# A fused decoder layer: one hand-written order of steps for all engines becomes one order for each engine, and an 8-bit cast moves from GpSimd to VectorE

## The reference, cut to what matters

```python
# x, ctx: (32, 256, 256); cells: (32, 1, 256, 1), integers 0..63
q, k, v = x @ Wq, x @ Wk, x @ Wv            # 16 query heads, 4 key/value heads, 64 wide
q, k = rope(q), rope(k)
a = softmax(q @ k.T / 8 + alibi)            # 16 heads, 256 x 256 each
x1 = layernorm(x + (a @ v) @ Wo)
# windowed cross attention: 16 heads of 16, windows of 64 looking one window back, cells must match
qx, kx, vx = proj(x1), proj(ctx), proj(ctx) # each with its own layernorm
o = softmax(where(mask, rope(qx) @ rope(kx).T / 4, -max)) @ vx
x2 = layernorm(x1 + proj(o))
# feed forward with ternary weights and activations rounded to 8 bits per token
h = gelu(quant8(x2) @ Wg.T) * (quant8(x2) @ Wu.T)
y = layernorm(x2 + quant8(h) @ Wd.T)
```

## Time and profile before

| | us |
|---|---|
| median of 3 runs (2417.35 to 2425.89) | 2421.6 |
| the profiled execution, its own time | 2430.4 |
| the profiled execution, its span | 2428.3 |
| TensorE busy in the span | 2162.9 (89%) |
| VectorE busy | 2030.8 (84%) |
| ScalarE busy | 1647.4 (68%) |
| GpSimd busy | 1500.9 (62%) |

### The profile page before, as it was taken

The page is one execution under the profiler, slowest core; times in us unless marked ns, Lnnn a source line. Parts: engine busy times, 40 slices in busy tenths (PEclk is TensorE's granted clock), DMA queues, the critical chain, the costliest instruction groups (busy, mean ns, idle before and its releaser), DMA issues. The chain is left out here.

```text
span 2428.3 us, 57742 instructions
## 1 busy us (share of the span) xinstructions
PE 2162.9 (89%) x19280; PEld 1652.3 (68%) x19370; DVE 2030.8 (84%) x8045; ACT 1647.4 (68%) x4609; POOL 1500.9 (62%) x1614
## 2 busy tenths in 40 slices
PE   4689999999999999999999999999999999999864
PEld 3566767677777767777776777777677777767642
DVE  4778788888888888888888888888888898888864
ACT  2366677776677777767777776777776677777642
POOL 2346566666766666666666666666666666666543
PEclk9899999999999999999999999999999999999986
DMA  3110010101110010111001001110100110010100
GB/s 99 61 30 25 19 36 25 34 25 28 34 34 25 26 34 25 28 34 34 25 26 34 25 27 34 34 25 26 34 25 27 34 34 25 26 34 23 29 14 9
DMA packets 85395, 74.62 MB, mean 31 GB/s; under 512 B 18544, under 2 KB 79344, under 8 KB 85104
## 3 DMA queue, kind: packets, MB, share of 16 engines
q1 hardware_dynamic: 85104, 70.93, 10.6%
HBM read 45.72 MB, written 8.39 MB: 22 GB/s over the span
## 5 line engine op out<-in xcount | busy, mean ns | idle before, releaser
L1152 ACT ACTIVATE prob<-prob,nmax 128x256 f32<-128x256 f32 x1024 | 508.5, 500 | 215.7 <-DVE nmax L879 215.5
L1240 POOL TENSOR_TENSOR prob<-prob,precs 128x512 f32<-128x512 f32 x512 | 524.0, 1042 | 200.3 <-DVE precs L886 197.8
L879 DVE CUSTOM_DVE_ANT_0 prob<-bank,alibi 128x256 f32<-128x256 f32 x1024 | 372.2, 420 | 51.7 <-PE bank L579 51.0
L475 PE MATMUL bank<-ident,prob 128*128 128x128 f32 x2048 | 315.8, 277 | 18.7 <-ACT pT L1159 13.9
L1159 ACT COPY pT<-bank 128x512 f32<-128x512 f32 x512 | 299.8, 586 | 40.0 <-PE bank L475 39.9
L1176 ACT ACTIVATE px<-px,nmx 128x128 f32<-128x128 f32 x1024 | 313.5, 391 | 19.1 <-DVE nmx L988 17.0
L475 PEld LDWEIGHTS bank<-ident,prob 128*128 128x128 f32 x2048 | 236.4, 141 | 81.5 <-issue 39.9
L598 PE MATMUL bank<-pT,v_sb 128*64 128x256 f32 x2048 | 252.0, 388 | 5.9 <-DVE xtok L899 5.2
L988 DVE CUSTOM_DVE_ANT_0 px<-bank,mask 128x128 f32<-128x128 f32 x1024 | 225.9, 286 | 20.0 <-PE bank L658 11.2
L487 PE MATMUL bank<-w_hi,x_hi 128*128 128x256 f32 (+1 forms) x512 | 193.3, 377 | 50.8 <-DVE by_sin L860 26.8
L1305 POOL TENSOR_SCALAR hq<-hh 128x1024 bf16<-128x1024 f32 x64 | 233.1, 3642 | 5.6
(11 more groups left out here) (209 smaller groups left out, 6042.6 us busy)
## 6 DMA issues: line engine op xcount, KB each, us to landing
raw<-in_xT SPq DMA_DIRECT2D x32, 256.0 KB, 2.7
kx_tok<-in_ctx SPq DMA_DIRECT2D x32, 256.0 KB, 3.0
xtok<-in_x SPq DMA_DIRECT2D x32, 256.0 KB, 2.8
raw<-in_ctxT SPq DMA_DIRECT2D x32, 256.0 KB, 3.4
kx<-k_sin SPq DMA_DIRECT2D x256, 32.0 KB, 2.0
vs<-vx SPq DMA_DIRECT2D x64, 128.0 KB, 2.3
out_y<-x SPq DMA_DIRECT2D x32, 256.0 KB, 2.1
cellk<-in_cell SPq DMA_DIRECT2D x32, 64.0 KB, 3.6
```

The lines of the kernel that those rows point to most:

```text
L475: last = nc.tensor.transpose(bank[:, n * P:(n + 1) * P], src, ident[:])
L879: v.tensor_tensor_reduce(out=prob[:, (2 * p + q) % SLOTS, c, :], in0=psum[SCORES[c]][:, q * L:(q + 1) * L], in1=alibi[:, p % 2, :], scale= ...
L1152: nc.scalar.activation(prob[:, (2 * p + q) % SLOTS, c, :], prob[:, (2 * p + q) % SLOTS, c, :], ACT.Exp, bias=nmax[:, i:i + 1], scale=-1.0, ...
L1240: g.tensor_tensor(prob[:, n % SLOTS, :, :], prob[:, n % SLOTS, :, :], precs[:, 2 * n:2 * n + 2].unsqueeze(2).to_broadcast([P, 2, L]), ALU. ...
```

## The change

1. `HEAD`, `BODY` and `TAIL` become dictionaries with one list for each of `sp`, `pe`, `dve`, `act`, `pool`. A step's part on one engine may now stand before or after another step's part, whatever the others do. `order(engine)` strings the three together; 27 repetitions of the body as before.
2. The order itself is new on every engine.
3. `HC`, the subtraction, clip and bf16 write of the second 8-bit rounding, is issued by VectorE.
4. The credits are gone: counts start at zero, and a wait on a batch that does not exist becomes a wait on a semaphore `begun` that GpSimd sets once.
5. ScalarE runs one `Exp` on four constants before its list.

The queries' rope (`Q`) and every other instruction stay as they are.

```diff
-CREDIT = 2
-BODY = [
-    (2, 'R', 12), (2, 'R', 13), (2, 'S', 7), (2, 'W', 0), (2, 'load_ctx'), (3, 'TX', 1, 1), (3, 'SX', 3), (2, 'mask'),
...
+BODY = {
+    "pe": [
+        (4, 'D', 0), (3, 'TX', 1, 1), (3, 'SX', 3), (2, 'O', 2), (3, 'OX', 0), (3, 'TX', 2, 0), (2, 'S', 7), (2, 'T', 12),
...
+        (2, 'NX'), (1, 'T', 3), (1, 'S', 3), (0, 'K'), (3, 'G', 1), (1, 'qT', 3), (2, 'QX'), (3, 'U', 1), (1, 'O', 0),
+        (2, 'KXT'), (3, 'G', 2), (1, 'T', 4), (3, 'U', 2), (0, 'Q', 0, 1), (1, 'T', 5), (1, 'S', 4), (3, 'G', 3),
+        (1, 'T', 6), (2, 'QXT'), (3, 'U', 3), (0, 'Q', 1, 1), (1, 'T', 7), (1, 'S', 5), (2, 'SX', 0), (1, 'O', 1),
+        (1, 'T', 8), (3, 'HT', 0), (1, 'T', 9), (2, 'SX', 1), (2, 'TX', 0, 0), (1, 'S', 6), (1, 'T', 10), (2, 'TX', 0, 1),
+        (1, 'W', 0), (2, 'SX', 2), (1, 'T', 11), (2, 'TX', 1, 0), (0, 'qT', 0),
+    ],
+    "dve": [
+        (2, 'R', 12), (3, 'SX', 2), (2, 'R', 13), (1, 'qT', 0), (4, 'D', 0), (3, 'SX', 3), (2, 'mask'), (4, 'HC', 1),
...
+        (2, 'YS'), (1, 'qT', 2), (3, 'U', 0), (1, 'S', 3), (2, 'NX'), (1, 'R', 6), (0, 'K'), (1, 'qT', 3), (1, 'R', 7),
+        (2, 'QX'), (3, 'U', 1), (2, 'KXT'), (3, 'HS', 0), (3, 'U', 2), (0, 'Q', 0, 1), (1, 'S', 4), (3, 'U', 3),
+        (2, 'QXT'), (1, 'R', 8), (1, 'O', 0), (1, 'S', 5), (3, 'HC', 0), (1, 'R', 9), (1, 'R', 10), (2, 'SX', 0),
+        (0, 'Q', 1, 1), (3, 'HS', 1), (1, 'O', 1), (1, 'R', 11), (2, 'SX', 1), (1, 'S', 6), (3, 'HT', 0), (1, 'W', 0),
+    ],
...
+HEAD = {
+    "sp": [
+        (0, 'first', 0), (0, 'first', 1), (0, 'first', 2), (0, 'loads', 1), (0, 'load_xT'), (0, 'load_ctx'),
+        (0, 'tables', 0), (0, 'loads', 0), (0, 'tables', 1), (1, 'load_xT'), (0, 'load_cell'), (0, 'loads', 2),
...
+    "dve": [
+        (0, 'first', 0), (0, 'first', 1), (0, 'first', 2), (0, 'prep', 0), (0, 'tables', 0), (0, 'K'), (0, 'Q', 0, 1),
+        (0, 'prep', 1), (0, 'prep', 2), (0, 'prep', 3), (0, 'Q', 1, 1), (0, 'kT'), (0, 'prep', 4), (0, 'qT', 0),
+        (0, 'qT', 1), (0, 'Q', 0, 2), (0, 'wo_split'), (0, 'Q', 1, 2), (0, 'prep', 5), (1, 'K'), (0, 'tables', 1),
+        (0, 'S', 0), (0, 'prep', 6), (0, 'R', 0), (0, 'R', 1), (0, 'S', 1), (0, 'R', 2), (0, 'prep', 7), (0, 'R', 3),
...
+FILL = max(x[0] for steps in BODY.values() for x in steps) + 1
+def order(engine):
+    return HEAD[engine] + [(it - lag, *step) for it in range(FILL, B) for lag, *step in BODY[engine]] + TAIL[engine]
+def freed(sem, bank, steps, n):
+    for batch, *step in reversed(steps[:n]):
         if holds(step[0], bank) or (step == ["prep", 5] and bank == 7):
             name, k = EMPTIED[tuple(step)]
-            return sem[name], (batch + CREDIT) * COUNT[name] + (k + 1)
-    return sem["x_hi"], 1
+            return sem[name], batch * COUNT[name] + k + 1
+    return sem["begun"], 1
...
         def at(name, batch, k=0):
-            return sem[name], (batch + CREDIT) * COUNT[name] + (k + 1)
+            count = batch * COUNT[name] + k + 1
+            return (sem[name], count) if count > 0 else (sem["begun"], 1)
...
-            for name, n in COUNT.items():
-                pe.sem_inc(sem[name], CREDIT * n)
             pe.wait_ge(pool_consts, POOL_CONSTS)
-            run(HEAD)
-            for it in range(FILL, LAST):
-                run(BODY, it)
-            run(TAIL)
+            run(order("pe"))
...
+                    elif kind == "HC":
+                        t, = args
+                        dve.wait_ge(*at("hq_shift", b, t))
+                        dve.wait_ge(*at("HT_mm", b, t - 1))
+                        v.tensor_scalar(hq[:], hh[:, t, :], MAGIC, 127.0, ALU.subtract, ALU.min).then_inc(sem["hq_ready"], 1)
...
+            act.wait_ge(pool_consts, 4)
+            nc.scalar.activation(psums[:, 0:1], minus_half[:, 0:1], ACT.Exp)
+            run(order("act"))
...
-                    elif kind == "HC":
-                        t, = args
-                        pool.wait_ge(*at("hq_shift", b, t))
-                        pool.wait_ge(*at("HT_mm", b, t - 1))
-                        g.tensor_scalar(hq[:], hh[:, t, :], MAGIC, 127.0, ALU.subtract, ALU.min).then_inc(sem["hq_ready"], 1)
...
+            pool.sem_inc(sem["begun"], 1)
```

More of the change, by code:

```diff
@@ L398, in one, with run @@
                 return ap[bass.ds(b, 1)]
-            def run(part, it=0):
-                for place, b, *step in batches(part, it):
+            def run(steps):
+                for place, (b, *step) in enumerate(steps):
                     kind, args = step[0], step[1:]
@@ L539, in run @@
                         pe.wait_ge(*at("x_lo", b))
-                        pe.wait_ge(*freed(sem, bank, part, place, it))
+                        pe.wait_ge(*freed(sem, bank, steps, place))
                         for t in range(TT):
@@ L1095, in _, with run @@
             dve.wait_ge(pool_consts, POOL_CONSTS)
-            run(HEAD)
-            for it in range(FILL, LAST):
-                run(BODY, it)
-            run(TAIL)
+            run(order("dve"))
         @block.scalar
         def _(act):
-            def run(part, it=0):
-                for place, b, *step in batches(part, it):
+            def run(steps):
+                for place, (b, *step) in enumerate(steps):
                     kind, args = step[0], step[1:]
@@ L1326, in _ @@
                                 pattern=[[-1, P]], channel_multiplier=1).then_inc(pool_consts, 1)
-            run(HEAD)
-            for it in range(FILL, LAST):
-                run(BODY, it)
-            run(TAIL)
+            run(order("pool"))
 def rope_table(n, dim, first):
```

109 lines of the change are left out of this document (60 added, 49 removed), and 270 rows, old and new, of tables (BODY, HEAD, TAIL).

## The result

The changed kernel takes 2326.2 us (median of 4 runs, 2325.2 to 2331.8), the kernel before 2423.7 beside it (4 runs, 2417.4 to 2426.2): ratio 0.961, 95% interval 0.958 to 0.963. The forecast was 2328. The profiled execution has a span of 2324.6 us where the one before had 2428.3, 103.7 us more.

The account below looks back on a forecast made before the run. TensorE and VectorE, both close to full, were taken to set the period through waits on each other or GpSimd. Body 73 + head 12 + tail 9 = 94 us off 2430.4 gives 2336, less 8.8: 2328 us, range 2285 to 2400.

Parts of the forecast that it names:

- The cast's price: HC on VectorE: 0.69 us per cast, 2 per batch, so 1.4 us more VectorE work per period.
- The hold of 0.3 us per period: VectorE's casts in the body, blocked by GpSimd instructions under way: 0.3 us per period taken, 2.5 at most.
- held by GpSimd: Rival: GpSimd always holds VectorE's cast, 58 us back, 2386 us; within the 2350 to 2410 group given 0.29.
- VectorE's busy time: Body, per period: 61.95 us plus 1.4 for the casts and 0.3 for their holding.
- TensorE's waits: Body: 4.7 us per period; HC's 1.56 and most others go, 0.9 stays (0.3 for xqT, 0.6 for XQ).
- VectorE's waits: Body: 7.3 us per period become about 3.9: ktok's 2.67 goes, W 0 costs 1.5, four others 0.6 each.
- The period: Body: 70.8 us falls to 68.0, from TensorE's 66.8 and VectorE's 68.85; gain 73 us, bounds 31 and 117.
- The head: Start and first batches: 12 us gained, between -12 and 30; first matmul at 17 us, 8 us from batches 1 to 5.
- The tail: Last batches, from 2271 us on: waiting for four casts mostly goes, 9 us gained, between 3 and 15.
- Sum: Whole kernel: 73 + 12 + 9 = 94 us gained, 2336 from the profiled 2430.4, 2328 as the runs' median.
- Slower: Rival in VectorE's body queue: it becomes the bound with waits unchanged, period 72.2 us, 2437 us; chance 0.09.
- No change: Rival: VectorE's waits of about 5.5 us per period, head and tail giving nothing; within 0.3%, chance 0.04.

Follow-up runs that it names:

- cast_only: The kernel before with only the cast HC moved from GpSimd to VectorE; common order, credits and start as before: 2457.6 us, ratio 1.014.
- cast_back: The changed kernel with HC back on GpSimd, directly behind HS in its list; all other orders as changed: 2409.4 us, ratio 0.994.
- mask_beside_pool: The changed kernel with the mask's four instructions moved directly behind HS 0 in VectorE's body list: 2400.9 us, ratio 0.990.
- cast_at_once: The changed kernel with each batch's first cast (HC 0) directly behind HS 0 in VectorE's body list: 2411.5 us, ratio 0.995.
- cast_behind_u: The changed kernel with each batch's first cast seven steps earlier on VectorE, behind HS 0 and U 2: 2359.5 us, ratio 0.973.

## Why the prediction was right

The time and the sign came out. The steps, in the prediction's order:

- **The cast's price.** Forecast 0.69 us from a line through two rows; measured 0.687 in the body. The hold of 0.3 us per period is not there in the kernel after, 24.7 us in 36 casts: its list puts the casts where GpSimd stands idle. One of the 64 began with a GpSimd instruction under way, outside the body, and took 1.54. The runs with the cast elsewhere show it in full, 1.52 us. So the rival *held by GpSimd* was not a matter of how busy GpSimd is, as I argued from a mean, but of one place in the list.
- **VectorE's busy time.** Forecast 61.95 + 1.4 + 0.3, measured 61.87. I had not seen that the mask's instructions, 2.14 us per period before, would be 1.07 after. Before, they ran beside a normalisation on GpSimd; below. Either half of the change ends that: they are short in cast_only and in cast_back as well.
- **TensorE's waits.** `hq` went, as forecast. `xqT` and `XQ`, for which I kept 0.9 us, went as well. In their place are 1.2 us for ScalarE's copies of `pT`, 0.4 for `qx` and 0.3 for `xtok`, which I didn't look for: I had set TensorE's list beside VectorE's, and not beside ScalarE's. 2.0 in place of 0.9.
- **VectorE's waits.** The `ktok` one went, 2.7 of the 7.3. The forecast of 1.5 us at `W 0` was wrong (0.1), and of the four of 0.6 at `D 1`, `SX 3`, `PO` and `KV 1` only 0.25 us at `SX` is there. Against that 2.0 us for scores and 1.9 for ScalarE's sums. 4.8 against 3.9, led by the scores and not by `W 0`, and 0.2 below the 5 that the prediction named as its own refutation.
- **The period.** 68.0 forecast, 68.2 measured, but the way to it was unsound: the mean of TensorE's 66.8 and VectorE's 68.85. Each engine's busy time, waits and short gaps fill one and the same period, so two sums that differ by 2 us mean that terms are wrong in one or both, and a mean does not mend them. TensorE's waits were put 1.1 us too low; VectorE's work 1.5 to 1.8 too high and its waits 0.9 too low. That these errors and the mean met at 68 was luck.
- **The head.** 12 us forecast, 26.0 measured, the term most off. The first matmul came at 14.25, not 17 (the load was issued at 4.01 and had landed by 12.04, not at 15). And for batches 1 to 5 I took 2 us less per batch; the starts of `kk_hi` are 66.3 us apart, where they were 72.0 before. The runs divide it: the start without credits gives 10 to 15, the common order kept but with the cast on VectorE takes 6 to 8, the separate orders give 17. The first scores come late, at 63.4 us (before 45.9), as forecast. The copy of batch 1's `V` is still 1.9 us later than before, and that of batch 2 is 15.7 earlier: 17.6 of the head's 26 us lie between these two.
- **The tail.** 9 forecast, 10.8 measured. **Sum:** 67 + 26 + 11 = 104, where 73 + 12 + 9 = 94 was forecast; the medians differ by 97.5, and the body's miss of 6 and the head's of 14 are opposite in sign. The time of 2328 came out by luck beyond that. The prediction took the gain from the profiled execution's 2430.4, which gives 2336, and then 8.8 off because the median before lay that much lower. After, the profiled execution took 2326.7 and the median is 0.5 below it. So the gain was 10 us too small and the 8.8 too large, and the two cancelled.
- ***Slower*.** I gave it 0.09 and put its place in VectorE's queue. The mechanism exists: cast_only is it, at 2457.6. VectorE's waits are 7.7 us per period there, above the 5.9 that the prediction named; it held them unlikely because the 2.67 for `ktok` go, which they did, and others came, 1.9 for ScalarE's `oT_hi` and 1.36 for `hh`. By TensorE's rows the loss in the body is the clock's, which the prediction has nowhere.
- ***No change*.** It put this at 5.5 us of waits. By its own floor it is 70.8 - 64.95 = 5.9, as under *slower*.

**How the change works**, by the runs: the cast on VectorE gives 36 us if it isn't put directly behind its own hand-over, and costs 33 if it is. The start gives 10 to 11. Separate orders give 55.8 and also a place for the cast. Orders and cast are not additive: with the cast on GpSimd, the new orders have TensorE wait for the normalisations behind it.

**Left open.** Whether the separate orders need the cast on VectorE: cast_back had it directly behind `HS` on GpSimd and nowhere else. Which of the remaining 2.0 us of TensorE's waits can be had; the 1.2 for `pT` are ScalarE's, and no run moved a single step of ScalarE. How the head's 17 us divide among the moved preparation steps wasn't tried. Nor was any engine's list put back alone with the others as they are, but for ScalarE's.

## What to carry to other kernels

Add up busy time and waits of the engine whose work the change leaves alone; the sum shows where a period's time went, and a rise of its busy time says to look at its clock. It closes for other engines as well, so it does not say who is the bound. For each instruction that is put on another engine ask two things: does it stand directly behind the step that hands its input away, and which step of the full engine waits for what is queued behind it. A part of a change that loses alone may be what makes the rest pay, so test it in a second place before it is dropped.

## What the runs showed of the hardware

**VectorE and GpSimd hold each other.** The mask in the kernel before, then in the kernel after:

```profile
820.90 2.04 POOL L1240 TENSOR_TENSOR prob<-prob,precs 128x512 f32<-128x512 f32 x2
821.47 0.50 DVE L972 CAST cellqf<-cellq 128x2 f32<-128x2 int32 x1
822.00 1.35 DVE L975 SCALAR_TENSOR_TENSOR mask<-cellk,cellqf,pen 128x128 f32<-128x128 int32 x2
```

```profile
1122.27 0.17 DVE L1100 CAST cellqf<-cellq 128x2 f32<-128x2 int32 x1
1122.47 0.61 DVE L1103 SCALAR_TENSOR_TENSOR mask<-cellk,cellqf,pen 128x128 f32<-128x128 int32 x2
```

0.50 against 0.17 us for a conversion of two columns, 1.35 against 0.61 for two of 128. GpSimd's scaling of `hh` was longer too, 1.28 beside the mask in mask_beside_pool and 1.12 elsewhere. Over the body this gave VectorE 1.07 us per period back, most of what the cast cost it. The cast at 1112.78 began 0.06 us behind a GpSimd instruction that ended at 1113.75, and ended itself at 1114.30, 0.55 later. Not every instruction is held: of the scores' in 18 periods of the trace before, 324 began with a GpSimd instruction under way and 252 did not, and both took 0.42 us in the median and 0.43 at most. By the Trainium skill ("SBUF — State Buffer", § SBUF: two separate sides) the one of the two engines that starts second is blocked for the whole instruction of the other, if VectorE's is in a two-port mode, or has two inputs in SBUF while GpSimd's reads SBUF. By that rule, the trace agrees, in what it shows held (casts, and the mask's operation with two inputs in SBUF) and in what not (the scores', with one of its inputs in PSUM).

**TensorE's clock can fall behind short waits.** A wait of 2.62 us, or two of 1.1 and 1.0 that end 2.1 us apart, was followed by stretches of 4 us at a granted 0.69 to 0.81, between the 2.4 and the 1.2 GHz level, and by an `O` of 3.54 us in place of 1.95. In cast_only that is 1.3 us per period on top of the waits, in cast_at_once as much. The fall came in 13 of 18 periods of the first and 16 of 18 of the second. Waits of up to 1.2 us by themselves, as in cast_behind_u and the kernel after, left the clock at 1.00. The kernel before has this pair in a period, and its clock stayed at 1.00 in the 4 us shown:

```profile
1012.27 0.62 PE L480 MATMUL bank<-ident,hq 128*128 128x128 bf16 x8 [1.55 <-POOL hq L1305]
...
1014.94 0.50 PE L487 MATMUL bank<-w_hi,x_hi 128*128 128x512 f32 x1 [1.03 <-DVE by_sin L860]
```

```profile
1012.00:1016.00 4.00, 2.70 (x21) 1.54 (x22) 2.40 (x9) 1.87 (x7) 2.52 (x3) 1.00 0.00 0
```

It stayed there in 15 of 18 periods and fell in 3. Waits of 1.8 to 1.9 us in cast_back were followed by a fall in 8 of 18. What sets the periods with a fall apart no run shows, so these counts are what happened and not a rule.
